# FFN second product with features on partitions, in a GNN block that keeps four engines busy

## What is computed

```python
h = relu(layernorm(x));  x = x + L0(h, adj)          # x: (8, 1024, 256)
h = relu(layernorm(x));  x = x + L1(h, adj)

# L0: deg * (h @ Wi.T + b) + adj @ (h @ Wj.T)
# L1: four attention heads over 1024 nodes (softmax of leaky(f1_i + f2_j) under the mask adj),
#     elu, a second attention layer with one head, elu -> out, and then the FFN that is changed here:
ffn = maximum(out @ w1 + b1, 0) @ w2 + b2            # 256 -> 256 -> 256
y = ffn + out
return (y - mean(y)) / sqrt(var(y) + 1e-5) * gamma + beta
```

## Time and profile before

| | |
|---|---|
| median of 3 runs | 1696.31 us (1692.17 to 1696.42) |
| the profiled execution | 1692.9 us, of which the span from first to last instruction is 1691.1 us |
| TensorE busy | 1564.2 us (92% of the span) |
| VectorE busy | 1456.0 us (86%) |
| ScalarE busy | 1377.5 us (81%) |
| GpSimd busy | 1001.9 us (59%) |
| mean granted clock of TensorE | 0.978 of full speed |

### The profile page before, as it was taken

One profiled execution on the slowest core, in us unless ns is written; L12 is line 12 of the kernel. 1 busy time (PEld: TensorE's weight loads), 2 busy tenths in 40 slices (PEclk: granted clock), 3 DMA queues, 4 the chain that ended last, 5 costly groups with the idle time before them and its releaser, 6 DMA issues.

```text
span 1691.1 us, 36352 instructions
## 1 busy us (share of the span) xinstructions
PE 1564.2 (92%) x13183; PEld 1315.1 (78%) x13184; DVE 1456.0 (86%) x2526; ACT 1377.5 (81%) x1862; POOL 1001.9 (59%) x1428
## 2 busy tenths in 40 slices
PE   5448999999999999999999999999999999998997
PEld 3336878788787887788787887878877888887876
DVE  4877699879999798988999799997989889898876
ACT  4177599879988798878997799887998789989972
POOL 4065367447675566656676476755766566686532
PEclk9779999999999999999999999999999999999999
DMA  8356498749987599767987599876998689788845
GB/s 267 75 139 112 101 199 156 121 90 188 186 147 115 122 182 173 131 101 159 206 139 123 97 189 184 145 116 124 183 173 129 101 138 184 123 134 131 136 76 100
DMA packets 780082, 240.87 MB, mean 142 GB/s; under 512 B 746624, under 2 KB 773376, under 8 KB 779776
## 3 DMA queue, kind: packets, MB, share of 16 engines
q1 hardware_dynamic: 772064, 231.18, 73.9%
q0 software_dynamic: 7840, 7.37, 3.8%
HBM read 38.01 MB, written 15.89 MB: 32 GB/s over the span
## 4 chain that ended last, share of the span: by engine, by line
PE 57%; DVE 13%; ACT 8%; issue 7%; DMA 6%; POOL 5%; SPq 3%; DVEq 0%; ACTq 0%; POOLq 0%
PE ps L130 10%; PE ps L1395 9%; PE ps L1401 9%; PE ps L1396 9%; PE ps L1415 6%; PE ps L139 5%; PE ps L1428 4%; DVE p_lo L1123 4%; PE ps L1476 2%; DMA pt_hi<-p_hi 2%; ACT p_hi L994 2%; DMA cat<-f_rows 2%; ACT xr L981 2%; DVE xr L1116 2%; SPq L860 2%
## 5 line engine op out<-in xcount | busy, mean ns | idle before, releaser
L1395 PE MATMUL ps<-pt_hi,hv_hi 128*128 128x256 f16 x2048 | 465.0, 274 | 33.3 <-DMA pt_hi<-p_hi 33.2
L1396 PE MATMUL ps<-pt_hi,hv_lo 128*128 128x256 f16 x2048 | 464.9, 274 | 0.0
L1123 DVE SCALAR_TENSOR_TENSOR p_lo<-xr,rden,p_hi 128x1024 f16<-128x1024 f32 x320 | 412.8, 1290 | 31.6 <-ACT p_hi L994 29.6
L994 ACT ACTIVATE p_hi<-xr,rden 128x1024 f16<-128x1024 f32 x320 | 366.6, 1146 | 39.3 <-POOL rden L903 37.9
L987 ACT ACTIVATE xr<-xr,shift 128x1024 f32<-128x1024 f32 x320 | 366.8, 1146 | 3.2 <-POOL shift L916 3.2
L901 POOL TENSOR_SCALAR den<-sums 128x1 f32<-128x1 f32 x320 | 154.3, 482 | 362.8 <-ACT xr L987 360.9
L1116 DVE CUSTOM_DVE_ANT_0 xr<-cat,mask_add 128x1024 f32<-128x1024 f32 x256 | 311.6, 1218 | 7.9 <-DMA cat<-f_rows 7.9
L981 ACT ACTIVATE xr<-xr,f1h 128x1024 f32<-128x1024 f32 x256 | 292.9, 1145 | 5.5 <-DVE mx L1116 5.5
L903 POOL TENSOR_TENSOR rden<-den,minus_one 128x1 f32<-128x1 f32 x320 | 265.2, 829 | 26.7
L1401 PE MATMUL ps<-pt_lo,hv_hi 128*128 128x256 f16 x2048 | 267.4, 274 | 1.7 <-DMA pt_lo<-p_lo 1.5
L914 POOL TENSOR_SCALAR zt<-mx,f1h 128x1 f32<-128x1 f32 x256 | 192.9, 754 | 115.5 <-DVE mx L1116 112.6
(11 more groups left out here) (199 smaller groups left out, 3126.8 us busy)
## 6 DMA issues: line engine op xcount, KB each, us to landing
cat<-f_rows SPq DMA_DIRECT2D x32, 512.0 KB, 4.5
out<-xx SPq DMA_DIRECT2D x28, 256.0 KB, 2.5
xx<-in_x SPq DMA_DIRECT2D x28, 256.0 KB, 3.4
out<-fin POOLq DMA_DIRECT2D x28, 256.0 KB, 5.3
pt_hi<-p_hi SPq DMA_TRANSPOSE x320, 3.3
pt_lo<-p_lo SPq DMA_TRANSPOSE x320, 3.3
adj_i<-in_adj SPq DMA_DIRECT2D x4, 1024.0 KB, 11.8
f2o<-f2o_rows SPq DMA_DIRECT2D x7, 512.0 KB, 4.2
```

The source lines that it names most:

```text
L994: nc.scalar.activation(p_hi[:, k % P_SLOTS, :], xr[:, k % X_SLOTS, :], ACT.Copy, scale=rden[:, k % 8:k % 8 + 1]).then_inc(hi_done, 1)
L1123: nc.vector.scalar_tensor_tensor(p_lo[:, k % P_SLOTS, :], xr[:, k % X_SLOTS, :], rden[:, k % 8:k % 8 + 1], p_hi[:, k % P_SLOTS, :], ALU.mu ...
L1395: nc.tensor.matmul(to, vh, hi, start=t == 0, stop=False)
L1396: nc.tensor.matmul(to, vl, hi, start=False, stop=False)
```

## The change

For all batches but the last, `ff2` now makes four products of 512 columns with w2 as the stationary operand, so that features stay on partitions, and drops the products with the identity. `y_out` becomes two instructions that add b2 (a column now) and `o2T`, and write back to `o2T`. A new TensorE step, `turn_y`, makes eight f32 transposes of 128x128 into psB. A new VectorE step, `norm_y`, holds the statistics and the old `gain`; it reads psB, and psB is free again only when it is done. The broadcast load of b2 goes. `w_head` moves from 4 steps behind its pair to 5, which puts it behind `project` in TensorE's list. The step tables get other numbers.

```diff
-G_HIGH, G_LOW, W_HEAD = 3, 4, 4
+G_HIGH, G_LOW, W_HEAD = 3, 4, 5
...
-                    sp.dma_start(b2_bc[:, :], b2.partition_broadcast(P)).then_inc(c_in, DMA)
...
-        FFN = ("ff1_0", "ff2_0", "ff1_1", "ff2_1")
+        FFN = ("ff1_0", "ff2_0", "turn_y0", "ff1_1", "ff2_1", "turn_y1")
-        STEADY = dict(load_x=-52, x_stats0=-47, x_stats1=-42, ... h0_low1=-34, ... m0=-31, m1=-30, m2=-29, m3=-28,
-                      ... x1_00=-24, x1_01=-23, x1_10=-22, x1_11=-22, ... f1T=-8, f1_out=-5, ...)
+        STEADY = dict(load_x=-52, x_stats0=-47, x_stats1=-41, ... h0_low1=-36, ... m0=-30, m1=-29, m2=-28, m3=-26,
+                      ... x1_00=-25, x1_01=-23, x1_10=-22, x1_11=-21, ... f1T=-9, f1_out=-4, ...)
-        SECOND = dict(... m3=-21, ... x1_rstd=-17, ... f1T=-7, f1_out=-6, ...)
+        SECOND = dict(... m3=-23, ... x1_rstd=-15, ... f1T=-6, f1_out=-6, ...)
-        CLOSING = dict(ff1_0=-1, hidden_0=1, ff2_0=2, y_0=4, rstd_0=5, gain_0=6, rescale_0=7, add_0=8, ff1_1=4, hidden_1=5, ff2_1=6, y_1=9,
-                      rstd_1=10, gain_1=11, rescale_1=12, add_1=13, save_f2o=-22, load_f2o=-16)
-        BESIDE_LAST = dict(ff1_0=-1, hidden_0=4, ff2_0=8, y_0=7, gain_0=8, rstd_0=10, rescale_0=16, add_0=14, ff1_1=9, hidden_1=8, ff2_1=9,
-                      y_1=11, rstd_1=14, gain_1=15, rescale_1=16, add_1=14, save_f2o=-21, load_f2o=-20)
+        CLOSING = dict(ff1_0=-2, hidden_0=0, ff2_0=1, y_0=2, turn_y0=3, norm_0=3, rstd_0=5, rescale_0=5, add_0=6, ff1_1=5, hidden_1=6,
+                      ff2_1=6, y_1=7, turn_y1=8, norm_1=9, rstd_1=11, rescale_1=12, add_1=15, save_f2o=-21, load_f2o=-20)
+        BESIDE_LAST = dict(ff1_0=-1, hidden_0=4, ff2_0=6, y_0=8, turn_y0=9, norm_0=10, rstd_0=10, rescale_0=13, add_0=14, ff1_1=7, hidden_1=9,
+                      ff2_1=11, y_1=11, turn_y1=12, norm_1=13, rstd_1=14, rescale_1=15, add_1=19, save_f2o=-22, load_f2o=-20)
...
-        LATE_ELU_EXP, LATE_ELU = K - U2 + 6, K - U2 + 7
+        LATE_ELU_EXP, LATE_ELU = K - U2 + 7, K - U2 + 8
...
-                return (ff_done if name[:3] == "ff1" else y_done), 2 * s + i + 1
+                return {"ff1": ff_done, "ff2": y_done, "tur": lny_gain}[name[:3]], 2 * s + i + 1
...
             def y_out(p, i):
-                nc.vector.tensor_tensor(y, general(which)..., b2_bc..., ALU.add).then_inc(y_done, 1)
-                (statistics as in norm_y below, from y)
+                for m in range(KF):
+                    part = o2T_of(p, i)[:, m, :]
+                    last = nc.vector.scalar_tensor_tensor(part, general(which)[:, m * 512:(m + 1) * 512], b2_col[:, m:m + 1], part, ALU.add, ALU.add)
+                last.then_inc(y_done, 1)
+            def norm_y(p, i):
+                which, seq = bank(f"turn_y{i}", p)
+                dve.wait_ge(bank_full[which], seq + 1)
+                turned = general(which)[:, :].rearrange("p (t f) -> p t f", f=F)
...
                 for t in range(half):
+                    last = nc.vector.bn_stats(stats_y[:, t, :], turned[:, t, :])
...
-            def gain(p, i):
...
+                    last = nc.vector.scalar_tensor_tensor(y_of(p, i)[:, t * F:(t + 1) * F], turned[:, t, :], mv_y[:, t, 0:1], gamma_bc[:, :], ALU.subtract, ALU.mult)
                 last.then_inc(lny_gain, 1)
...
             def ff2(p, i):
+                for m in range(KF):
+                    last = product(to[:, m * 512:(m + 1) * 512], [(w2_sb[:, k, m * P:(m + 1) * P], ff_half[:, k * 512:(k + 1) * 512]) for k in range(KF)])
+                last.then_inc(full, 1)
+            def turn_y(p, i):
+                to, full = open_bank(f"turn_y{i}", p)
+                pe.wait_ge(y_done, 2 * p + i + 1)
                 for t in range(half):
                     for k in range(KF):
-                        nc.tensor.matmul(to[:, t * F:(t + 1) * F], ff_half[...], w2_sb[:, k, :], start=k == 0, stop=False)
-                        last = nc.tensor.matmul(to[...], o2T_of(p, i)[:, k, tok], ident[:, :], start=False, stop=k == KF - 1)
+                        last = nc.tensor.transpose(to[:, t * F + k * P:t * F + (k + 1) * P], o2T_of(p, i)[:, k, t * P:(t + 1) * P], ident[:, :])
                 last.then_inc(full, 1)
```

More of the change, by code:

```diff
@@ L700, in build @@
         HEADS = ("rows", "f1T")
-        FFN = ("ff1_0", "ff2_0", "ff1_1", "ff2_1")
[L702 to L706, removed]
-                      load_cat=-7)
@@ new lines, in build @@
+        STEADY = dict(load_x=-52, x_stats0=-47, x_stats1=-41, x_rstd=-40, x_norm0=-39, h0_high0=-39, h0_low0=-38, h0_high1=-37, h0_low1=-36,
+                      turn_h0_0=-38, turn_h0_1=-34, m0=-30, m1=-29, m2=-28, m3=-26, mj_high0=-30, mj_high1=-28, mj_high2=-27, mj_high3=-26,
+                      mj_low0=-29, mj_low1=-28, mj_low2=-27, mj_low3=-25, x1_00=-25, x1_01=-23, x1_10=-22, x1_11=-21, x1_out0=-22,
+                      x1_out1=-20, save_x1=-20, x1_stats0=-22, x1_stats1=-17, x1_rstd=-16, x1_norm0=-15, hv_high0=-15, hv_low0=-14,
+                      x1_norm1=-14, hv_high1=-14, hv_low1=-14, turn0=-14, turn1=-14, rows=-11, rows_out=-11, f1T=-9, f1_out=-4, save_f2=-8,
+                      load_cat=-7)
@@ new lines, in build @@
+        SECOND = dict(load_x=-45, x_stats0=-32, x_stats1=-32, x_rstd=-31, x_norm0=-31, h0_high0=-29, h0_low0=-29, h0_high1=-28, h0_low1=-26,
+                      turn_h0_0=-29, turn_h0_1=-25, m0=-27, m1=-25, m2=-24, m3=-23, mj_high0=-26, mj_high1=-25, mj_high2=-23, mj_high3=-21,
+                      mj_low0=-25, mj_low1=-24, mj_low2=-23, mj_low3=-20, x1_00=-21, x1_01=-20, x1_10=-17, x1_11=-17, x1_out0=-18,
+                      x1_out1=-17, save_x1=-19, x1_stats0=-17, x1_stats1=-17, x1_rstd=-15, x1_norm0=-15, hv_high0=-15, hv_low0=-13,
+                      x1_norm1=-13, hv_high1=-13, hv_low1=-12, turn0=-13, turn1=-12, rows=-9, rows_out=-9, f1T=-6, f1_out=-6, save_f2=-9,
+                      load_cat=-7)
@@ L721, in build @@
+        QUARTERS = dict(ff1=(-4, -2, 2, 2), hidden=(-4, -2, 2, 6), ff2=(1, 1, 2, 4), y=(1, 2, 4, 5), turn=(1, 1, 5, 9), norm=(2, 3, 5, 5),
+                      rstd=(2, 4, 4, 10), rescale=(3, 5, 7, 7))
         SPREAD_F2 = first2[B - 2] + U2 - 1
-        LATE_ELU_EXP, LATE_ELU = K - U2 + 6, K - U2 + 7
+        LATE_ELU_EXP, LATE_ELU = K - U2 + 7, K - U2 + 8
         ADD_BETA = first1[B - 1] + 5
@@ L1230, in y_out @@
                 dve.wait_ge(bank_full[which], seq + 1)
-                y = y_of(p, i).rearrange("p (t f) -> p t f", f=F)
-                nc.vector.tensor_tensor(y, general(which)[:, :].rearrange("p (t f) -> p t f", f=F), b2_bc[:, :].unsqueeze(1).to_broadcast([P, half, F]), ALU.add).then_inc(y_done, 1)
-                hold(dve, "dve", y_done, 2 * p + i + 1)
+                for m in range(KF):
[6 more added lines that the diff above has]
+                turned = general(which)[:, :].rearrange("p (t f) -> p t f", f=F)
+                if 2 * p + i:
+                    dve.wait_ge(lny_done, 2 * p + i)
                 for t in range(half):
-                    last = nc.vector.bn_stats(stats_y[:, t, :], y[:, t, :])
+                    last = nc.vector.bn_stats(stats_y[:, t, :], turned[:, t, :])
                 last.then_inc(lny_stats, 1)
@@ L1357, in _ @@
                             y_out(s, i)
-                        if due(n, s, f"gain_{i}"):
-                            gain(s, i)
+                        if due(n, s, f"norm_{i}"):
+                            norm_y(s, i)
                         if due(n, s, f"rescale_{i}"):
@@ L1553, in _ @@
                             ff2(s, i)
+                        if due(n, s, f"turn_y{i}"):
+                            turn_y(s, i)
                 for q in quarter_due(n, "ff1"):
```

16 lines of the change are left out of this document (3 added, 13 removed).

## The result

The median of the changed kernel is 1719.22 us (1716.37 to 1723.08) against 1695.37 of the kernel before: ratio 1.0145, 95% interval [1.0118, 1.0173]. Slower was forecast, but by 8 us; 24 us is past the end of the range, 1714. The profiled execution's span is 1715.5 us against 1691.1. The first fence holds a line of the page of the changed kernel (busy us and share of the span), the second the same stage as in the earlier trace rows.

The account below looks back on a forecast made before the run. TensorE was taken as the bound, with VectorE nearly full at the anchor. Five closings +9, `W_HEAD` +2, closing 5 -1 and batch 6's save -2 gave +8 on 1692.9, plus 3.4 to the median: 1704 us, range 1681 to 1714.

Parts of the forecast that it names:

- the term for `W_HEAD`: At every pair `w_head` comes 1.31 us later, behind `project`; priced at +2 us in all (0 to 9).
- The anchor: Closings beside a front: VectorE work ahead of `g_low` c0 stalls TensorE; +1.8 us a batch, +9 over five.
- The stall: TensorE at `w_head` c0 waits 3.6 us for `g_low`, which VectorE ends at 1075.7.
- the first half's saving: First ff2 half of a closing: 0.77 us of TensorE saved, but swallowed by the wait at `w_head` c0.
- the worst case of a batch: Closing beside a front: +4 us if VectorE's idle times stay and no hand-off wait is won.
- rival C: At psB, ff1_1 and the m products wait for late `norm_0`; 1710 to 1718 us, chance 0.07.
- TensorE's products: ff2 half: products 3.43 us plus transposes 1.04, against 5.24 before; saves 0.77, or 10.8 over 14 halves.
- Rival D: Closing transposes without overlap: eight take 2.16 us, a half 0.35 more than before; 1712 us, chance 0.03.
- Rival A: At the anchor VectorE's added work is covered, so the saving counts; 1679 to 1685 us, chance 0.34.
- Batch 7: Start of batch 7: batch 6's earlier f2o save shortens TensorE's wait for the load; -2 us (0 to -4.9).
- The last closing: Step-table edits `SECOND`, `QUARTERS`, `LATE_ELU`, add and rescale: 0 us, each with 3 either way.

Follow-up runs that it names:

- run 2: Kernel before the change with W_HEAD set to 5 alone: 1710.75 us, 1.0097.
- run 4: Changed kernel with W_HEAD still 5, but in the odd step TensorE makes `w_head` ahead of `project`: 1702.43 us, 1.0043.
- run 5: Changed kernel with 12 unread products added at c13 while TensorE waits for `ht_low`: 1715.56 us, 1.0114.
- run 10: Run 4 with the eight transposes of the first half made twice in `turn_y`: 1702.40 us, 1.0048.
- run 11: Run 4 with the front's first layernorm steps and transposes later in STEADY, `h0_high1` behind the normalisation it reads: 1695.07 us, 1.0009.
- run 3: Changed kernel with the old front tables `STEADY` and `SECOND`: 1750.78 us, 1.0328.
- run 9: Kernel before the change with `save_f2o` of batch 6 at -22 in place of -21: 1691.56 us, 0.9981.
- run 6: Run 4 with `x_stats1` of the front and `y_0` of batch 6 each one step sooner: 1704.55 us, 1.0054.
- run 1: Changed kernel with W_HEAD back at 4, nothing else: 1719.75 us, 1.0143.
- run 7: Run 4 with `norm_0` behind `g_low` c0 and what follows it in the closing one step later: 1708.21 us, 1.0074.

## Why the forecast was wrong

**The step that failed** is the term for `W_HEAD`: "1.31 us later ... where ScalarE comes close behind, some 0.3 in each of seven batches: +2 (0 to 7 x 1.31 = 9)". I priced the later `w_head` by who waits for it, and too low: between c13 and c14 `ht_low` comes 1.2 us later where I had put 0.3 in a batch. And I didn't ask what it had been covering, which the forecast so put at nothing. VectorE is busy all the time there, `w_head` was the work that TensorE did while it waited for `ht_low`, and the rows of the kernel before (0.16 and 0.38 us idle) hardly look like a wait, because the cover took up the rest. Swapped behind the wait it leaves 3.2 us idle, the clock falls, and a period loses 4.1 us, some 3.2 after what is given back: 19.4 us in six periods against my upper bound of 9. Runs 2 and 4 show it from both sides; run 5 shows that 1.6 of the 4.1 are the clock.

**The anchor** was right in mechanism; that its size came out near, +9 forecast for five closings and +6.9 measured in the changed kernel, is in part luck. The stall itself is 2.3 us, not 3.6, which with the forecast's other terms would have left 5 x 0.5 = 2.5; where the other 4.4 come from is not settled. The stall is smaller by three errors of one sign. From `p_lo` of unit E to the end of `g_low` c0 VectorE took 1090.91 - 1064.32 = 26.6 us (27.06 forecast; `y_out` 1.40 and `norm_y` 3.75, near the 1.4 and 3.8 of the sum). From ff1_0 to its arrival at `w_head`, 1090.97 - 2.33 = 1088.64, TensorE took 26.2 (1072.1 - 1046.5 = 25.6 forecast). And ff1_0 started 1.85 ahead of that `p_lo`, not 2.13. Run 10 shows that the first half's saving is swallowed there, and run 11 that taking the VectorE work away from ahead of `g_low` gives back some 7 us. One sum of the forecast was off: by its own rows the worst case of a batch is 1077.6 - 1072.19 - 0.8 = +4.6, not +4, so rival C should have reached 1720. The measured time lies near that, but C's cause, a wait of the m products for `norm_y`, is in no row of the changed kernel; only run 3 has it.

**TensorE's products.** The ff2 half takes the time of ff1 (3.67 us for the eight products of each), and eight transposes 1.04 us from start to end, the forecast's own number, at 0.87 us for eight in a row (in run 10, behind sixteen of them, `attend` c1 starts 1.75 us after the first). So a half saves 5.24 - 3.43 - 0.87 = 0.94, a little more than forecast, and 14 halves 13 us; in run 11 TensorE is busy 1552.1 us, 12.1 less than before. Rival D is out. The instruction's mean of 273 ns is what the Trainium skill gives in "TensorE: Matmul & The Clock Gate", Part 4 (PE-mode transpose), some 275 ns (for bf16; here it is f32); the trace agrees with that as the length of one, but eight in a row stand 0.11 apart, so it is no price per transpose.

**Rival A** needed the stall away. Run 11 has that, and the order put right, and still doesn't win 11 us: it is level with the kernel before. The saving was made there (12.1 us of busy time, above), and TensorE is idle 13.2 us longer instead. From 300 to 1500 us its waits grew by 10.4 us: 3.9 for the elu ahead of ff1_0 (7.8 in place of 3.9), 3.3 for `g_low`, 2.9 for `hidden_1`, 1.0 for `pt_hi`, and less than 1 each for `ht_low` and `pt_lo`, against 2.1 less at m. So in run 11 the work that TensorE was spared turned into waits, most of them for VectorE and ScalarE.

**The smaller terms.** Batch 7: -2 forecast, -4.4 measured; run 9 shows the save to be worth 3 us by itself in the kernel before, of which I had counted the wait and not the clock behind it. Whether the -4.4 are the save's is open: run 4 has it too and gains 3.6 there, although its wait at the place is 5.03 us, longer than the 4.87 of before. The last closing: 0 within 3 forecast, +2.7 measured, with one wait of 5.0 us at ff1_1 for `y_0`; run 6 shows only that moving `y_0` by one step turns it into other waits. What those of batch 6's steps cost one by one stays open.

## What to carry to other kernels

In an in-order list a step that is moved behind another is priced by two questions: who waits for it, and which wait it was filling. Where an engine's waits look like 0.2 us, look at what stands between them and add it up, above all in stretches that another engine bounds. And when an experiment undoes an edit and the time stays, read its waits before dropping the theory: run 1 removed 18 us of one wait and bought 11 of two others and 8 of a third.

## What was not expected of the hardware

Idle times of TensorE of the same length had different ends. 3.21 us between c13 and c14 of the changed kernel were followed by some 3 us at a granted clock of 0.50, in each of six periods, and cost 1.65 us beyond themselves. In run 2 the idle time at that place is 3.76 us in all six, and behind two of them the clock stayed at 1.00. Ahead of `attend` c10 of batch 7, 3.29 us in run 9 left it at 1.00 (run 9's row above), and 3.29 us in run 7 did not:

```profile
1556.72 0.27 PE L1398 MATMUL ps<-pt_hi,hv_hi 128*128 128x256 f16 x1 [3.29 <-DMA pt_hi<-p_hi]
```

```profile
1558.00:1559.00 1.00, 1.00 (x6) 0.76 (x5) 1.00 (x2) 1.00 (x2) 0.90 (x2) 0.50 1.09 294
```

Shorter ones can do it too: in the kernel before, 2.57 us ahead of `attend` p2 of the second period were followed by 0.50, and 2.33 us at the same place of the fifth were not. Among these, from 2.33 to 3.76 us, the length alone doesn't tell whether the clock falls. What else decides the runs don't show, so the cost of a fall that one trace has is no sure part of the time of the next execution.
